# First layer of a decoder: cross attention divided in token rows, packed by pairs of heads, and router logits in four column tiles

## What is computed

```python
x = x + L0_attn(layernorm(x))            # causal linear attention, 16 heads of 16
x = x + L0_xattn(layernorm(x), ctx, mask)
x = x + L0_ffn(layernorm(x))             # 16 experts, top 2, capacity 640

# L0_xattn: ctx has 77 keys for each of the 16 sequences
q = (x @ wq) * 16 ** -0.5; k = ctx @ wk; v = ctx @ wv      # 16 heads of 16
weights = softmax(q @ k.T + mask)                           # over the 77 keys
x_out = (weights @ v) @ wo

# L0_ffn, its router
logits = x @ gate_w.T                                       # 16 experts
vals, sel = top_k(sigmoid(logits), 2)                       # then rank of each token in its expert
```

## Time and profile before

| | |
|---|---|
| time, median of 3 runs | 1675.9 us (1675.7 to 1676.32) |
| span of the profiled execution | 1668.4 us |
| PE busy | 1538.6 us, 92% |
| DVE busy | 979.4 us, 59% |
| ACT busy | 843.9 us, 51% |
| POOL busy | 466.9 us, 28% |

### The profile page before, as it was taken

The page is one execution under the profiler, slowest core; times in us unless marked ns, Lnnn a source line. Parts: engine busy times, 40 slices in busy tenths (PEclk is TensorE's granted clock), DMA queues, the critical chain, the costliest instruction groups (busy, mean ns, idle before and its releaser), DMA issues. The chain is left out here.

```text
span 1668.4 us, 27286 instructions
## 1 busy us (share of the span) xinstructions
PE 1538.6 (92%) x10207; PEld 1083.6 (65%) x10207; DVE 979.4 (59%) x2295; ACT 843.9 (51%) x1849; POOL 466.9 (28%) x592
## 2 busy tenths in 40 slices
PE   8999999998987899999999999999999989996299
PEld 5777767766755677778777556665666654442288
DVE  3665766767766435222222666767665568777883
ACT  4456555555555422211122565666656633597980
POOL 4213234253234320000001665555533300032100
PEclk9999999999999999999999999999999979998599
DMA  3440111111151144443444211111100000000031
GB/s 116 157 156 18 47 30 44 30 47 44 34 166 39 56 148 125 140 132 114 126 126 127 80 39 52 32 41 31 39 14 11 4 26 1 0 1 16 23 100 64
DMA packets 100929, 108.32 MB, mean 65 GB/s; under 512 B 25410, under 2 KB 89804, under 8 KB 100800
## 3 DMA queue, kind: packets, MB, share of 16 engines
q1 hardware_dynamic: 94656, 90.01, 17.2%
q0 software_dynamic: 6144, 16.57, 3.1%
HBM read 64.77 MB, written 42.01 MB: 64 GB/s over the span
## 5 line engine op out<-in xcount | busy, mean ns | idle before, releaser
L1789 POOL TENSOR_SCALAR c_pr<-c_pr,c_rsum 128x256 f32<-128x256 f32 x256 | 127.3, 512 | 185.0 <-DVE c_rsum L2205 184.7
L2083 ACT ACTIVATE c_pr<-bank,c_nmax 128x256 f32<-128x256 f32 x256 | 117.8, 472 | 118.4 <-DVE c_nmax L2200 118.3
L1520 ACT ACTIVATE b_G<-bank 128x320 f32<-128x320 f32 x128 | 55.9, 437 | 210.0 <-PE bank L1469 210.0
L1469 PE MATMUL bank<-b_XT,shared 128*128 128x320 f32 x512 | 154.2, 436 | 0.0
L2200 DVE TENSOR_REDUCE c_nmax<-bank 128x2 f32<-128x512 f32 x128 | 82.4, 685 | 104.1 <-PE bank L1848 104.0
L1483 PE MATMUL bank<-shared,b_G 128*128 128x256 f32 x640 | 142.2, 379 | 0.0
L1483 PEld LDWEIGHTS bank<-shared,b_G 128*128 128x128 f32 x640 | 121.2, 190 | 17.5
L1066 DVE TENSOR_TENSOR hT_all<-bank,a_causal 128x512 f32<-128x512 f32 x128 | 79.4, 682 | 68.4 <-PE bank L561 68.4
L496 POOL TENSOR_TENSOR a_L<-a_L,a_Lm 128x1232 f32<-128x1232 f32 x32 | 71.9, 2247 | 153.9 <-DVE a_Lm L1081 153.9
L1469 PEld LDWEIGHTS bank<-b_XT,shared 128*128 128x128 f32 x512 | 92.4, 192 | 27.3 <-issue 1.0
L1539 DVE COPY b_Y<-bank 128x256 f32<-128x256 f32 x80 | 33.9, 424 | 120.3 <-PE bank L1483 120.1
(11 more groups left out here) (375 smaller groups left out, 3420.6 us busy)
## 6 DMA issues: line engine op xcount, KB each, us to landing
shared<-L_ffn_w SPq DMA_DIRECT2D x32, 512.0 KB, 6.1
t_slots_in<-a_h SPq DMA_DIRECT2D x20, 512.0 KB, 7.4
shared<-t_slots_in SPq DMA_DIRECT2D x15, 640.0 KB, 7.1
t_slots_out<-b_Y SPq DMA_DIRECT2D x15, 640.0 KB, 4.1
hT_all<-x SPq DMA_DIRECT2D x8, 512.0 KB, 3.9
a_xr<-x SPq DMA_DIRECT2D x8, 512.0 KB, 3.8
t_x_a<-a_x SPq DMA_DIRECT2D x8, 512.0 KB, 2.8
shared<-t_x_a SPq DMA_DIRECT2D x8, 512.0 KB, 3.8
```

The lines of the kernel that those rows point to most:

```text
L1469: t = p.matmul(P[2 + n % 2][:, 0:HC], w1[e % 3][:, u, 128 * f:128 * f + 128], XT[e % 2][:, u, HC * m:HC * m + HC], start=(u == 0), stop=(u ...
L1789: p.tensor_scalar(pr[k][:, e, u, :], pr[k][:, e, u, :], rsum[k][:, e, u:u + 1], 1.0, ALU.mult, ALU.mult).then_inc(q.pr_ready, 1)
L2083: a.activation(pr[t % 2][:, e, u, :], P[e][:, S * u:S * u + S], ACT.Exp, bias=nmax[t % 2][:, e, u:u + 1], accum_out=sums[t % 2][:, e, u:u ...
```

## The change

Cross attention is divided by its sum before the transposes, in token rows. After `exponents`, VectorE sums `L` over the keys and takes the reciprocal (`sums`); GpSimd multiplies (`normalised`) and writes the first 64 keys of each head into `Pm` and the last 13 into `Pl`. Two heads of 64 keys fill 128 partitions, eight heads of 13 keys fill 104, so a tile has eight transposes from `Pm` and two from `Pl` in three units instead of 16 in four. The values are laid out to match: `xvp` holds a pair of heads as a block-diagonal 128 x 32, `xvl` the last keys of eight heads as a masked 104 x 128. `x_values` now adds two full-width matmuls and eight in column tiles in one bank, and its result is already in the form that `project` reads. The transposes back and forth (`xtok`, `xcol`) and `divide` fall away. For the values of the context there are two products instead of one: `xvm` (two matmuls) and `xvl` (four), the latter from `ctxl`, which ScalarE fills (`repeat_tail`). The logits are eight matmuls of 128 x 32 against 128 columns in four column tiles, `gate` is one transpose. `masked` no longer waits for the transposes of the tile before last but for its `normalised`.

Cut to what the prediction speaks of:

```diff
-        UNITS = {0: (("xtok0", -3), ("xtok1", -3), ("k0", 1), ("k1", 1), ("tok2", -1), ("tok3", -1), ("xq1", -2)),
-                 1: (("val0", 0),) + tuple((n, -3) for n in turned(3)) + (("col1", -1), ("xcol0", -3), ("xk", -1), ("v0", 1)),
-                 2: (("proj1", -1), ("xproj0", -3), ("xval1a", -3), ("xval1b", -3), ("pkt", 1)),
-                 3: (("val1", 0),) + tuple((n, -2) for n in turned(0)) + (("xtok2", -3), ("xtok3", -3), ("turn2a", -4), ("turn2b", -4), ("xv", -1)),
-                 4: (("tok0", 0), ("tok1", 0), ("q0", 1), ("q1", 1), ("xcol1", -3), ("logits", -4)),
-                 5: (("val2", 0),) + tuple((n, -2) for n in turned(1)) + (("col0", 0), ("xproj1", -3), ("v1", 1), ("gate", -4)),
-                 6: (("proj0", 0), ("turn1a", -1), ("turn1b", -1), ("xval0a", -2), ("xval0b", -2), ("turn0a", 2), ("turn0b", 2),
-                     ("rank", -4), ("state0", 1), ("state1", 1)),
-                 7: (("val3", 0),) + tuple((n, -2) for n in turned(2)) + (("xq0", -1),)}
+        UNITS = {0: (("k0", 1), ("k1", 1), ("tok2", -1), ("tok3", -1), ("xq1", -2)) + tuple((n, -3) for n in turned(2)),
+                 1: (("val0", 0), ("col1", -1), ("xproj0", -3), ("xk", -1), ("v0", 1)),
+                 2: (("proj1", -1), ("pkt", 1)) + tuple((n, -3) for n in turned(3)),
+                 3: (("val1", 0), ("turn2a", -4), ("turn2b", -4), ("xval1", -3), ("xvm", -1), ("xvl", -1)),
+                 4: (("tok0", 0), ("tok1", 0), ("q0", 1), ("q1", 1), ("logits", -4)) + tuple((n, -2) for n in turned(0)),
+                 5: (("val2", 0), ("col0", 0), ("xproj1", -3), ("v1", 1), ("gate", -4)),
+                 6: (("proj0", 0), ("turn1a", -1), ("turn1b", -1), ("turn0a", 2), ("turn0b", 2),
+                     ("rank", -4), ("state0", 1), ("state1", 1)) + tuple((n, -2) for n in turned(1)),
+                 7: (("val3", 0), ("xq0", -1), ("xval0", -2))}
...
+                def normalised(i, j):
+                    n = NT * i + j
+                    p.wait_ge(q.xden_ready, n + 1)
+                    if n:
+                        wait_full(p, f"xt{(n - 1) % NT}_{NTURN - 1}", (n - 1) // NT)
+                    p.tensor_tensor(Pm[:, :, :], L[n % 2][:, :, 0:KM], bcast(xrden[:, j, :], 2, KM), ALU.mult).then_inc(q.xn_ready, 1)
+                    p.tensor_tensor(Pl[:, :, :], L[n % 2][:, :, KM:S2], bcast(xrden[:, j, :], 2, KL), ALU.mult).then_inc(q.xn_ready, 1)
...
                     if s in (0, 1) and there(g - 5):
                         scatter(g - 5, s)
+                    if s == 1 and there(g - 3):
+                        normalised(g - 3, 3)
...
+                    if s == 3 and there(g - 2):
+                        normalised(g - 2, 0)
...
+                    if s == 5 and there(g - 2):
+                        normalised(g - 2, 1)
...
+                    if s == 7 and there(g - 2):
+                        normalised(g - 2, 2)
...
                 def x_turn(i, j):
...
-                    p.wait_ge(q.exp_ready, n + 1)
-                    for rg in range(RG):
-                        name = f"xt{j}_{rg}"
+                    p.wait_ge(q.xn_ready, 2 * n + 2)
+                    for u in range(2):
+                        name = f"xt{j}_{u}"
                         room(p, name, i)
-                        for k in range(4):
-                            x = p.transpose(bank(name, i)[0:S2, 128 * k:128 * k + 128], L[n % 2][:, 4 * rg + k, :], ident)
+                        for r in range(4):
+                            x = p.transpose(bank(name, i)[:, 128 * r:128 * r + 128], Pm[:, 8 * u + 2 * r:8 * u + 2 * r + 2, :].rearrange("p h k -> p (h k)"), ident)
...
+                    for u in range(2):
+                        p.matmul(bank(name, i)[:, S * u:S * u + S], xvl[i % 2][:, b, u, :], PTl[:, u, :], start=(u == 0), stop=False,
+                                 skip_group_check=True)
+                    for u in range(2):
+                        for r in range(4):
+                            x = p.matmul(bank(name, i)[32 * r:32 * r + 32, S * u:S * u + S], xvp[i % 2][:, b, 4 * u + r, :], PTm[:, 4 * u + r, :],
+                                         start=False, stop=True, tile_position=(0, 32 * r), skip_group_check=True)
...
                     for u in range(2):
-                        x = p.matmul(bank("logits", i)[0:E, :], wg[:, u, :], hT2[:, u, :], start=(u == 0), stop=(u == 1))
+                        for j in range(NT):
+                            x = p.matmul(bank("logits", i)[32 * j:32 * j + 32, 0:128], wg[:, u, :], hT2[:, u, 128 * j:128 * j + 128],
+                                         start=(u == 0), stop=(u == 1), tile_position=(0, 32 * j), skip_group_check=True)
...
                     if n >= 2:
-                        wait_full(v, f"xt{(n - 2) % NT}_{RG - 1}", (n - 2) // NT)
+                        v.wait_ge(q.xn_ready, 2 * n - 2)
...
+                def sums(i, j):
+                    n = NT * i + j
+                    v.wait_ge(q.exp_ready, n + 1)
+                    v.tensor_reduce(xrden[:, j, :], L[n % 2][:, :, :], AX.X, ALU.add).then_inc(q.xsum_ready, 1)
+                    v.wait_ge(q.xsum_ready, n + 1)
+                    v.reciprocal(xrden[:, j, :], xrden[:, j, :]).then_inc(q.xden_ready, 1)
```

228 lines of the change are left out of this document (122 added, 106 removed).

## The result

The changed kernel takes 1713.1 us (median of 4 runs, 1709.3 to 1716.2) against 1675.8 for the kernel before: ratio 1.0233, 95% interval 1.0218 to 1.0248. It is 37 us slower; the forecast was 18 us slower, with a range that ended at 1704. The sign was right, and so was what bounds the full group steps; the size was half of what came, and the price of the drain was wrong in its parts.

The account below looks back on a forecast made before the run. VectorE's chain, held by GpSimd, was taken to bound the stretch from gate to `x_scores` of tile 0, TensorE the rest of a full group step. From 1675.9, −.2 to group step 8 and +18 for the drain gave 1694 us; range 1663 to 1704.

Parts of the forecast that it names:

- The chain from the gate's end to T1: Full group step, gate's end to `x_scores` of tile 0 (T1): VectorE, held by GpSimd, makes it 30.1 us, +5.1.
- TensorE's saving: Full group step: fewer transposes and cheaper logits, less added context work, take 6.0 to 6.6 us off TensorE's busy time.
- The rule on tile modes: `x_values`: changing tile mode drains the array; under 2 us a group on TensorE, left out of the sum.
- no `weigh` under a subtraction yet: Group steps 2 to 4: `weigh` not yet held by GpSimd's subtraction, so they gain 1.8, 2.5 and 3.5 us.
- the −3.0 from T1 to the gate: From `x_scores` of tile 0 to the next gate, where TensorE leads: 40.0 us becomes 37.0.
- −.2 and +1.9: Sum to the start of group step 8, −.2 us; then `x_scores` of tile 0 in group step 8, +1.9.
- rival E: Drain: as the likeliest case, but waits drop TensorE to its lower clock about eight times, +10 us: 1704; chance .13.
- the drain's price: Drain: its three pieces lose 5.9, 7.3 and 3.2 us; with +1.9 ahead of them, some +18.
- four times 9.4 is 37.5 for the 29.8: Drain, `x_scores` of tile 0 to tile 3: each tile's chain takes 9.4 us instead of 7.4, +7.3.
- B: Full steps: `choose` isn't held, three steps cost 2.1 us less each, drain +10: about 1679; chance .20.
- C: Full steps: VectorE isn't held at all, three steps 3.7 us faster each, drain +8: 1666; chance .17.
- D: Whole kernel: TensorE is the bound throughout, −51 us with the drain's loss hidden: 1625; chance .08.

Follow-up runs that it names:

- `idle_products`: Kernel before, plus two GpSimd products per group step on a buffer that nothing reads: 1707.3 us, ratio 1.0203.
- `less_first`: Changed kernel with GpSimd's order swapped: subtraction of tile 2 ahead of product of tile 1, that of tile 3 ahead of product of tile 2: 1690.5 us, ratio 1.0112.
- `own_wait`: Changed kernel with a semaphore of their own for the router's weights, so the first matmuls don't wait for them: 1712.8 us, ratio 1.0248.
- `norm_early`: Changed kernel with the second four scattered writes issued behind the product of tile 3, not ahead of it: 1703.3 us, ratio 1.0190.
- `keep_clock`: Changed kernel with idle TensorE transposes ahead of long waits in the drain, to keep its clock up: 1711.5 us, ratio 1.0230.
- `sums_first`: Changed kernel with VectorE's sum of a tile ahead of the masking of the next one, all work the same: 1670.7 us, ratio .9983.

## Why the prediction was half right

**Right: what bounds the kernel.** The chain from the gate's end to T1 was worked out as 30.1 us instead of 24.95; from the gate's start, as I measure it here, it is 31.6 instead of 25.2: +6.4 where I had +5.1. Its terms: `M` at +4.5 (measured: 326.09, that is 4.5 behind the gate's 321.56), `x_scores`(3) at some +12 (11.6), `weigh` with its holds 6.5 (338.74 to 345.52, 6.8). The difference is the last term, `xq1`, which I took at its 1.72 us though I had put a wait ahead of it: it ran at the lower clock and took 3.34. In group step 4, where it did not, gate to T1 is 30.6. `idle_products` and `less_first` show that the holds cause it and do not only stand beside it: 34 us for work that nobody needs, 20 back for an order (two thirds of it holds, by group step 5). The Trainium skill, "SBUF — State Buffer", "Who interferes with whom", describes the shared ports of VectorE and GpSimd as an exclusive lock held for the whole instruction; the traces agree to a tenth of a microsecond (`slot` ends at the seam each time in the full steps).

**Right: TensorE.** T1 to the gate was 40.0 and should be 37.0; it is 36.6, from 39.8. TensorE's saving of 5.4 us for a step is a little under the 6.0 to 6.6, and the waits before `xq1` (3.68 us) are where they were put. The rule on tile modes that I weighed made no visible difference: `x_values` takes 1.03 + 1.07 us for a sequence, as summed.

**Where the other 21.5 us are.** 3.2 at the start, −.9 up to group step 4, 9.8 from there to T1 of 8 (14.9 instead of 5.1), 9.4 in the drain. The start is not shown to be real (`own_wait`). The others are these.

**Wrong: group step 4 (4.5 us).** I let it gain 3.5, "no `weigh` under a subtraction yet". The step that failed is this count. It has one: the router of g − 4 is that of group 0 there, and the trace shows `oh` at 256.34 with 2.33 us and `slot` at 272.28 with 1.89. Group step 4 costs 64.8 us, 1.0 more than before. That is an error of counting, in code that stood in front of me.

**Wrong: the gain of group step 7 (4.3 us).** I took the −3.0 from T1 to the gate for every step. In group step 7 nothing of two groups ahead is left to do, TensorE doesn't lead, and that stretch takes 33.5 us (T1 at 419.25 to the gate at 452.75) where it took 32.2. Some of it is the clock again: the three blocks from T1 on take 4.3 us instead of 2.4, at the lower level behind a wait of 5.04. The +6.0 of the stretch ahead of it (29.5 for 23.5) stands without its discount. With the start, T1 of group step 8 is 13.7 us late where my sum had −.2 and +1.9.

**Wrong: the clock, a term that the sum had at nothing.** I kept the lower clock out of the sum and looked for it in the drain alone, as rival E. It came in the full group steps too, granted clock .93 against .99: 1.5 us between gate and T1 behind group step 5, 1.9 of the 4.3 in group step 7.

**Wrong: the drain's price (+16.4 told, +25.8 measured).** The pieces: T1 to T1 7.4 (told 5.9), T1 to `x_scores` of tile 3 11.1 (7.3), from there to the last projection 7.5 (3.2). The mechanism, tile 3 behind eight writes, is right (`norm_early`, 7 to 10 us back). The count is not. From T1 in s1 to `x_scores` of tile 3 in s7 are three tile steps, not four. So "four times 9.4 is 37.5 for the 29.8" (+7.7, where the text says +7.3) came near by luck; three times 9.4 would have been a gain, and 15 for tile 3 with two of 9.4 is 33.8. Measured are 16.8, 10.1 and 14.0 us, for 9.1, 13.1 and 7.6 in the kernel before.

The first holds a wait for tile 3, the 11.73 us, which I had put into the pieces before and behind this one. The second is the plain tile, 10.1 for my 9.4. The third holds TensorE's wait for `M`, 5.00 us at 564.49, which I did not count at all. VectorE's sum and masks are not its cause, they were over when the gate came. From the gate's end (559.48) to the end of `M` (564.43) are 4.95 us, 2.5 in the kernel before; the rest is `oh` held 2.0 us and the cast ahead of it .3. And the kernel before had `x_values` between gate and ranks, 1.94 us of work under that chain (531.99); the change moved it to s7. The last transposes of tile 3 wait 10.57 us once more, which in my sum of the tail was only 3.2. I had taken two tile steps in a row for independent; where each one waits for the last, every hold and each sum is paid in full.

**The other cases.** The lower clock, which I put at 10 us of the drain in rival E, stays open: some 5 us more than in the kernel before by the estimate under `keep_clock`, and that run can't decide it. Rivals B (`choose` not held), C (not held) and D (TensorE the bound) are out for this kernel; but `sums_first` shows how near C's world was: one line's place in VectorE's loop decides between 61.6 and 68 us a step. Two slips of a tenth or of one us in the prediction (VectorE's net is +4.6 by its own terms, and 8 x 6.5 is 52) change nothing. The range ended at 1704 since it was built on E and my own sum; the doubt about the drain, a stretch with no pattern to count by, should have widened it.

## What to carry to other kernels

Before moving work to GpSimd, look at what VectorE does at that minute: in these runs short SBUF-to-SBUF instructions cost VectorE the rest of GpSimd's instruction, while its reads of PSUM and its reductions took no longer. Put the new work beside those, and try the order of the same instructions before changing their number. Count by hand in which steps of a pipeline each piece exists, first and last steps too; price the drain as a chain, with all of the new latency in it, as nothing there lies beside it. Price the block behind a long wait of TensorE at both levels of its clock, and where idle work is put into such waits, count what it delays in the places that don't wait.
